# Attention and feed-forward block on one core: units that begin with denominators, and earlier projections for the next batch

## The chip, the cores and the metric

The kernel runs on one core of one Trainium2 chip. The metric is the device time of one execution in microseconds (us), lower is better; before the change the median of three runs is 1805.7 us. The engines are named as the profile names them: PE (TensorE matmuls), PEld (its weight loads), ACT (ScalarE), DVE (VectorE), POOL (GpSimd) and SP (SyncE, which here only issues DMAs).

## What is computed

Eight batches of 1024 tokens with 256 features, 16 heads of 16 features. Cut to what matters, for each batch:

```python
qkv = layernorm(x) @ Wqkv;  q, k, v = split(qkv)           # 16 heads of 16 features
num = exp(rope(q) @ rope(k).T * scale)                      # rotated queries and keys
den = sum(exp(q @ k.T * scale), axis=-1)                    # PLAIN queries and keys, all 1024 columns
attn = where(causal, num / den, 0)
x = x + (attn @ v) @ Wout + bout
x = x + squared_relu(layernorm(x) @ Ws1) @ Ws2 + routed experts(layernorm(x))
```

Numerator and denominator use different scores, so each head needs two score matrices: one from rotated projections (only its causal part) and one from plain ones (all of it). The routed experts get a truncated probability; when the count of tokens with a non-zero one is 0, their loop is skipped.

## The kernel before

**Units and steps.** The work is cut into 32 units: 8 batches (`b`), each with 4 groups of four heads (`g` = 0 to 3, here units one to four of a batch). A unit has 50 steps, written down in `STEPS`. A step is one score tile of 128 x 1024: PE computes it into one of three PSUM tiles (`RING = 3`) and ACT takes its exponential. There are 32 denominator steps, `("den", j, i)` (two matmuls of 512 columns in `scores_step`, the sum along the row by ACT's accumulator), and 18 numerator steps, `("num", c, j)`, in five chunks `c` (four steps each, the last chunk two). PE may compute the tile of step n when ACT has finished that of step n-3 (`exp_done`). Everything is ordered by hand with semaphores; every engine runs its own program in order.

**Side work of PE.** After the score tile of a step PE may do a piece of attention times v (`PV_STEPS`: the step of each of the 12 pieces, function `heads_step`) and one tile of other work (`SIDE`: per unit, step -> kind). The kinds are `v` (value projection), `qk` (projection of the next unit's queries and keys: tiles 0 and 2 are the plain projections of the two halves of the tokens, 1 and 3 the matmul with a swap matrix that the rotation needs), `xt`, `t2` (transposes), `norm`, `acc`, `route`, `ffn`. Tiles in `IN_TWO` take two steps in a row. All side tiles share one PSUM bank, so each waits until DVE has taken the one before (`taken`).

**How queries and keys reach PE.** DVE and POOL split each projected tile into three bf16 parts (`qk_tile` on DVE, `low_part` on POOL, which stands `LOW_LAG = 3` steps behind in POOL's program and sets `low_ready`). SP sends the parts to a scratch tensor in HBM (`send_parts`, `qk_parts<-parts`) and from there fills a stack of 96 rows in SBUF (`fill_stacks`, 12 DMAs for the plain kind and 12 for the rotated kind, `stack<-qk_parts`). There are two stacks by parity of the unit. One semaphore for each parity, `stacked`, counts all 24 fills, and PE waits for all of them ahead of the first step of a unit.

**Order in a unit before.** Four numerators (chunk 0), 7 denominators, chunk 1, 7 denominators, chunk 2, 6, chunk 3, 6, chunk 4, 6 denominators. The next unit's projections run as side work of the present unit; in unit four of a batch they are those of the next batch.

**Outputs.** `send_out(b, g)` waits for `out_ready` and sends two blocks of `x_mid`. Before, the first of a batch stood in SP's program between the two halves of `send_parts`, the second behind its fills, the other two at the end of the batch.

Of the kernel before, what the change touches and what calls it, by code (L numbers as in the profile page):

```python
# [25 lines left out]
HG = 4  # L26
# [10 lines left out]
RING = 3  # L37
Q_TERMS = (0, 0, 0, 1, 1, 2)
K_TERMS = (0, 1, 2, 0, 1, 0)
FILLS = 2 * 2 * TERMS  # L40

# [16 lines left out]

def unit_steps():
    steps, dens = [], [("den", j, i) for j in range(HG) for i in range(NB)]
    for c, count in zip(range(5), (7, 7, 6, 6, 6)):
        steps += [("num", c, j) for j in (range(HG) if c < 4 else range(0, HG, 2))]
        steps += [dens.pop(0) for _ in range(count)]
    return steps

# [2 lines left out]
NSTEP = len(STEPS)  # L70
LAST_STEP = {c: max(s for s, x in enumerate(STEPS) if x[:2] == ("num", c)) for c in range(5)}
FIRST_DEN = next(s for s, x in enumerate(STEPS) if x[0] == "den")

PIECES = [(0, 0), (0, 1), (1, 0), (1, 1), (2, 0), (2, 1), (2, 2), (3, 1), (3, 0), (3, 2), (4, 0), (4, 1)]
PV_STEPS = [
# [4 lines left out]
]  # L82
PV_AT = [dict(zip(steps, PIECES)) for steps in PV_STEPS]
CHUNK_END = [(0, 1), (1, 1), (2, 2), (3, 2), (4, 1)]
# [10 lines left out]


SIDE = [
    {0: ("v", 0), 4: ("v", 1), 9: ("qk", 0), 13: ("v", 2), 16: ("qk", 1), 19: ("qk", 2), 26: ("qk", 3),
     28: ("v", 3)},
    {0: ("qk", 0), 7: ("qk", 1), 11: ("qk", 2), 18: ("qk", 3), 24: ("norm", 0), 26: ("norm", 1),  # L100
     28: ("acc", 0), 29: ("acc", 1), 35: ("acc", 2), 38: ("acc", 3)},
    {0: ("qk", 0), 5: ("t2", 0), 7: ("qk", 1), 8: ("t2", 1), 11: ("qk", 2), 15: ("t2", 2), 17: ("qk", 3),
     19: ("t2", 3), 24: ("route", 0), 25: ("route", 1), 28: ("norm", 0), 31: ("norm", 1), 35: ("acc", 0),
     37: ("acc", 1), 39: ("route", 2), 41: ("acc", 2), 44: ("acc", 3)},
    {0: ("xt", 0), 3: ("xt", 1), 5: ("xt", 2), 8: ("xt", 3), 11: ("qk", 0), 16: ("ffn", 0), 18: ("qk", 1),
     21: ("ffn", 1), 23: ("qk", 2), 28: ("ffn", 2), 31: ("qk", 3), 34: ("ffn", 3), 36: ("ffn", 4),
     38: ("ffn", 5), 41: ("ffn", 6), 45: ("ffn", 7)},
]
IN_TWO = {("v", 0), ("v", 1), ("v", 2), ("v", 3), ("qk", 0), ("qk", 2)}
FFN = [("up", 0), ("up", 1), ("down", 0), ("up", 2), ("down", 1), ("up", 3), ("down", 2), ("down", 3)]  # L110
# [19 lines left out]
def block(nc, x, w_qkv, w_out, b_out, ws1, ws2, w1, w2, wr, cos_in, sin_in, out):  # L130
# [5 lines left out]
    with ExitStack() as ctx:  # L136
# [6 lines left out]
        def sem(name):  # L143
            return ctx.enter_context(nc.semaphore(name))
# [117 lines left out]
        @program.sync  # L262
        def _(sp):
            w_qkv_v = w_qkv.rearrange("(k p) n -> p k n", p=P)
            sp.dma_start(x_in[:, :, :], x_v[0]).then_inc(x_loaded, 16)
            sp.dma_start(stage, w_qkv_v[:, :, 0:2 * D]).then_inc(loaded, 16)
            sp.dma_start(cos_sb[:, :], cos_in).then_inc(tables_loaded, 16)
            sp.dma_start(sin_sb[:, :], sin_in).then_inc(tables_loaded, 16)
            sp.dma_start(w_v[:, :, :], w_qkv_v[:, :, 2 * D:3 * D]).then_inc(more_loaded, 16)
            wo_v = w_out.rearrange("(p a j d) n -> a j d p n", p=2, a=2, j=HG)  # L270
            for a in range(2):
                for j in range(HG):
                    sp.dma_start(w_o[32 * j + DH * a:32 * j + DH * (a + 1), :, :], wo_v[a, j]).then_inc(more_loaded, 16)
# [5 lines left out]
            def send_parts(b, g, outs=None):  # L279

                parity = g % 2

                if not (isinstance(b, int) and b == 0 and g == 0):
                    sp.wait_ge(stacked[1 - parity], at(b, 2 * FILLS * 16, (g + parity) // 2 * FILLS * 16))
                    sp.sem_inc(held["sp"], 1)
                for half in range(2):
                    for kind, sent in ((0, plain_sent), (1, rot_sent)):
                        sp.wait_ge(low_ready, at(b, 16, 4 * g + 2 * half + kind + 1))
                        sp.sem_inc(held["sp"], 1)
                        sp.dma_start(scratch[kind, :, :, :, half * HALF:(half + 1) * HALF].rearrange("c s r t -> (s r) c t"),  # L290
                                     parts[:, kind, :, :]).then_inc(sent, 16)
                        if half == 1:
                            if kind == 0 and not (isinstance(b, int) and b == 0 and g < 2):

                                sp.wait_ge(scores_ready, at(b, G * NSTEP, (g - 1) * NSTEP))
                                sp.sem_inc(held["sp"], 1)
                            fill_stacks(b, g, kind, sent)
                    if outs is not None:
                        send_out(outs, half)

            def fill_stacks(b, g, kind, sent):

                parity = g % 2
                sp.wait_ge(sent, at(b, 8 * 16, 2 * 16 * (g + 1)))
                sp.sem_inc(held["sp"], 1)
                src = scratch[kind].rearrange("c s (d h) t -> c s d (h t)", h=HG)
                for a, terms in enumerate((Q_TERMS, K_TERMS)):
                    for term, part in enumerate(terms):
                        sp.dma_start(stack[term:ROWS:TERMS, parity, kind, a, :], src[part, a]).then_inc(stacked[parity], 16)  # L309

            def batch(b, first, last):
                for g in range(G):
                    if g < G - 1:
                        send_parts(b, g + 1)
                    elif not last:
                        send_parts(b + 1, 0, None if first else b - 1)
# [166 lines left out]
        def _(pe):  # L483
# [139 lines left out]
            def experts(b):  # L623
# [4 lines left out]
                with pe.If(count > 0):  # L628
                    with pe.Fori(0, E) as e:
                        base = at1(b, TILES["gen"], 0) + e * 12  # L630

# [62 lines left out]
            def batch(b, first, last):  # L694

                before = [("qk", b, 3)] + ([] if first else [("ffn", b - 2, TILES["ffn"] - 1)])
                for g in range(G):
                    parity = g % 2
                    pe.wait_ge(stacked[parity], at(b, 2 * FILLS * 16, (g // 2 + 1) * FILLS * 16))
                    for s, step in enumerate(STEPS):  # L700
                        scores_step(b, first, g, s, step)
                        if s in PV_AT[g]:
                            heads_step(b, first, g, s)
                        before = side_step(b, first, last, g, s, before)
                        if (g, s) == BRANCH and not first:

                            for k0, b0, n0 in before:
                                pe.wait_ge(taken[k0], at(b0, TILES[k0], n0 + 1))
                            experts(b - 1)
                            before = before + [("gen", b - 1, TILES["gen"] - 1)]  # L710


# [6 lines left out]
            pe.wait_ge(more_loaded, 16 * MORE_LOADS)  # L719
            batch(0, True, False)  # L720
            with pe.Fori(1, B - 1) as b:
                batch(b, False, False)
# [378 lines left out]
```

## Time and profile before

| | |
|---|---|
| Median of 3 runs | 1805.7 us (1805.3 to 1807.01) |
| The profiled execution | 1806.99 us, its span 1805.4 us |
| ACT busy | 1600.0 us, 89% of the span |
| PE busy | 1543.6 us, 85% |
| DVE, POOL busy | 46%, 28% |
| DMA, mean busy share of 16 engines | 30%, 96 GB/s |
| ACT in the chain that ended last | 22%, PE 27%, issue 31% |

Times in the rows are microseconds, unless marked ns. In a timeline a row is a start, a length, the engine, the source line, the instruction, its output and input with their shapes, and a count of instructions that were merged; the square bracket is how long the engine had been idle and what ended the idle time. The length of a merged matmul row contains the end of the last matmul's pipeline, so what a piece of PE work costs is read from start to start. PEclk is the clock granted to TensorE as a share of full speed: 1.00 is 2.4 GHz, 0.50 is 1.2 GHz.

### The profile page before, as it was taken

To read this page: it belongs to the slowest core of one execution; us is meant where nothing else is said; L and a number is where in the kernel's file an instruction comes from. 1 tells how busy PE (TensorE), PEld (TensorE's weight loads), DVE (VectorE), ACT (ScalarE), POOL (GpSimd) and SP (SyncE) were. 2 spreads that over 40 slices of the span, in tenths; PEclk is the share of its full clock that TensorE was granted. 3 is DMA by queue.
4 is the path that set the end of the run, shared out by engine and by line. 5 is a ranking of instruction groups with operands and counts; after the bars stand their busy time and mean duration, and the time that the engine had idled before them with its cause. 6 is when DMAs were issued, how large, how long until landed. Compare 5 with 4: busy or idle time off the path is not lost.

```text
span 1805.4 us, 29587 instructions
## 1 busy us (share of the span) xinstructions
PE 1543.6 (85%) x8416; PEld 612.0 (34%) x8416; DVE 825.3 (46%) x1824; ACT 1600.0 (89%) x2633; POOL 506.5 (28%) x868
## 2 busy tenths in 40 slices
PE   2688889889898898889988988988988889888985
PEld 1222324233433334233432333433443333423333
DVE  5232433464335653365533644347533565336315
ACT  0599998999899998999979998899989999899990
POOL 3133232231233221332322323224123322133210
PEclk8799999999999999999989999999999999999997
DMA  3234232332333313333223323233133331333300
GB/s 114 88 106 125 91 106 73 103 103 71 122 105 106 117 36 115 111 121 100 83 80 100 120 88 120 83 109 110 58 121 105 124 110 42 105 106 97 97 24 24
DMA packets 95023, 172.44 MB, mean 96 GB/s; under 512 B 15488, under 2 KB 82048, under 8 KB 82560
## 3 DMA queue, kind: packets, MB, share of 16 engines
q1 hardware_dynamic: 94848, 170.33, 30.2%
q8 instruction: 82, 1.34, 0.3%
q14 instruction: 93, 0.76, 0.1%
HBM read 111.55 MB, written 58.72 MB: 94 GB/s over the span
## 4 chain that ended last, share of the span: by engine, by line
issue 31%; PE 27%; ACT 22%; POOL 9%; DVE 6%; SPq 2%; DMA 2%; DVEq 0%; ACTq 0%; POOLq 0%
ACT scores L458 14%; PE scores L500 7%; ACT probs L468 7%; PE y_ps L529 5%; PE scores L507 4%; POOL parts L381 4%; PE side L559 3%; POOL rot L379 3%; SPq L309 2%; PE side L566 2%; POOL x_acc L409 1%; PE side L539 1%; ACT probs L470 1%; PE side L580 1%; PE side L614 1%
## 5 line engine op out<-in xcount | busy, mean ns | idle before, releaser
L458 ACT ACTIVATE scores<-scores 128x1024 f32<-128x1024 f32 x1024 | 1046.7, 1028 | 28.6 <-PE scores L500 27.3
L500 PE MATMUL scores<-stack 96*128 96x512 bf16 x2048 | 584.3, 386 | 59.8 <-ACT probs L468 26.3
L468 ACT ACTIVATE probs<-scores 128x1024 f32<-128x1024 f32 x512 | 490.4, 1026 | 119.2 <-PE scores L507 117.2
L507 PE MATMUL scores<-stack 96*128 96x512 bf16 (+3 forms) x1536 | 335.9, 334 | 89.1 <-DMA stack<-qk_parts 68.6
L529 PE MATMUL y_ps<-probs,v_sb 128*32 128x512 f32 (+3 forms) x3072 | 332.6, 505 | 5.9 <-ACT probs L468 4.8
L371 POOL TENSOR_SCALAR_AFFINE_SELECT probs<-probs 128x256 f32<-128x256 f32 (+1 forms) x640 | 224.7, 378 | 372.9 <-ACT probs L468 219.0
L500 PEld LDWEIGHTS scores<-stack 96*128 96x128 bf16 x2048 | 161.2, 98 | 430.5 <-ACT scores L458 202.2
L507 PEld LDWEIGHTS scores<-stack 96*128 96x128 bf16 x1536 | 124.4, 98 | 357.7 <-ACT scores L458 143.8
L381 POOL TENSOR_TENSOR parts<-rest,parts 128x512 bf16<-128x512 f32 x128 | 148.0, 1156 | 344.8 <-DVE parts L813 338.6
L379 POOL TENSOR_TENSOR rot<-raw,cos_sb 128x512 f32<-128x512 f32 x64 | 90.0, 1407 | 515.3 <-DVEq L826 515.3
L458 ACT ACTIVATION_READ_ACCUMULATOR scores<-scores 128x1 f32 x1024 | 206.2, 201 | 0.0
L559 PE MATMUL side<-xnt,w_qk 128*128 128x512 f32 x248 | 126.8, 592 | 0.0
L825 DVE COPY raw<-side 128x512 f32<-128x512 f32 x62 | 42.9, 691 | 159.5 <-PE side L559 148.8
L529 PEld LDWEIGHTS y_ps<-probs,v_sb 128*32 128x32 f32 x3072 | 60.8, 108 | 144.6 <-issue 116.4
L831 DVE TENSOR_TENSOR rest<-side,sin_sb 128x512 f32<-128x512 f32 x62 | 42.7, 690 | 100.8 <-PE side L566 100.8
L793 DVE COPY v_sb<-side 128x128 f32<-128x128 f32 x128 | 28.2, 283 | 124.5 <-PE side L539 123.5
L863 DVE COPY y_sb<-y_ps 128x512 f32<-128x512 f32 x32 | 21.9, 685 | 137.0 <-PE y_ps L529 137.0
L566 PE MATMUL side<-parts,swap 128*128 128x512 bf16 x186 | 52.1, 389 | 33.5 <-POOL parts L381 23.4
L539 PE MATMUL side<-w_v,xnt 128*128 128x256 f32 x256 | 78.1, 434 | 0.0
L809 DVE TENSOR_TENSOR rest<-raw,parts 128x512 f32<-128x512 f32 x64 | 71.9, 1124 | 5.2 <-issue 0.5
L580 PE MATMUL side<-w_o,y_sb 128*128 128x256 f32 x240 | 63.7, 387 | 2.6 <-DVE x_mid L882 2.5
L470 ACT ACTIVATE probs<-scores 128x1024 f32<-128x1024 f32 x64 | 63.0, 1036 | 1.4 <-PE scores L507 1.3
(110 smaller groups left out, 1116.9 us busy)
## 6 DMA issues: line engine op xcount, KB each, us to landing
stack<-qk_parts SPq DMA_DIRECT2D x768, 128.0 KB, 2.6
qk_parts<-parts SPq DMA_DIRECT2D x128, 384.0 KB, 2.6
x_in<-in_L_attn_x SPq DMA_DIRECT2D x8, 1024.0 KB, 5.5
out<-x_mid SPq DMA_DIRECT2D x32, 256.0 KB, 2.8
probs<-in_L_attn_Wqkv SPq DMA_DIRECT2D x1, 512.0 KB, 6.7
cos_sb<-in_cos SPq DMA_DIRECT2D x1, 512.0 KB, 7.4
sin_sb<-in_sin SPq DMA_DIRECT2D x1, 512.0 KB, 8.3
w_v<-in_L_attn_Wqkv SPq DMA_DIRECT2D x1, 256.0 KB, 8.0
```

What stands on the lines that cost most here:

```text
L371: nc.gpsimd.affine_select(out=v, in_=v, compare_op=ALU.is_ge, fill=0.0, base=0, pattern=pattern, channel_multiplier=-1).then_inc(masked, 1)
L379: nc.gpsimd.tensor_tensor(rot[:, :], raw[:, :], cos_sb[:, t // 2 * HALF:(t // 2 + 1) * HALF], ALU.mult)
L381: nc.gpsimd.tensor_tensor(parts[:, t % 2, 2, :], rest[:, :], parts[:, t % 2, 1, :], ALU.subtract).then_inc(low_ready, 1)
L458: nc.scalar.activation(src, src, ACT.Exp, scale=SCALE, accum_out=den[:, g % 2, i, j:j + 1]).then_inc(exp_done, 1)
L468: nc.scalar.activation(probs[:, chunk % 2, j, :], src, ACT.Exp, scale=SCALE).then_inc(exp_done, 1)
L500: mm = nc.tensor.matmul(tile[:, half * HALF:(half + 1) * HALF], q[:, j, i * P:(i + 1) * P], k[:, j, half * HALF:(half + 1) * HALF], start= ...
L507: mm = nc.tensor.matmul(tile[:, col:col + n], k[:, h, i * P:(i + 1) * P], q[:, h, q0:q0 + n], start=True, stop=True)
L529: mm = nc.tensor.matmul(y_ps[32 * j:32 * j + 32, o0:o0 + n], v_sb[:, i, h, :, :], probs[:, (5 * g + c) % 2, j, col:col + n], start=piece i ...
L539: mm = nc.tensor.matmul(side[:, i * D:(i + 1) * D], xnt[:, k, (2 * t + i) * P:(2 * t + i + 1) * P], w_v[:, k, :], start=k == 0, stop=k == ...
L559: mm = nc.tensor.matmul(side, w_qk[:, k, g, :], xnt[:, k, half * HALF:(half + 1) * HALF], start=k == 0, stop=k == KC - 1)
L566: mm = nc.tensor.matmul(side, swap[:, :], parts[:, 0, i, :], start=i == 0, stop=i == PARTS - 1)
L580: mm = nc.tensor.matmul(side[:, i * D:(i + 1) * D], y_sb[:, pair, (2 * t + i) * P:(2 * t + i + 1) * P], w_o[:, pair, :], start=True, stop= ...
```

## The change

`FILLS` counts the fills of one stack (12), and each kind and parity has its own semaphore. PE waits for the plain stack ahead of a unit's first denominator and for the rotated stack ahead of its first numerator. The unit's order becomes 7 denominators, the 8 numerators of chunks 0 and 1, 7 denominators, and from there as before; only steps 0 to 10 differ. The pieces of chunks 0 and 1 in `PV_STEPS` and most of `SIDE` are moved. SP sends all four outputs behind the fills. The waits ahead of the experts' branch stand inside the branch.

```diff
-FILLS = 2 * 2 * TERMS
+FILLS = 2 * TERMS
...
-    for c, count in zip(range(5), (7, 7, 6, 6, 6)):
-        steps += [("num", c, j) for j in (range(HG) if c < 4 else range(0, HG, 2))]
+    for chunks, count in zip(((), (0, 1), (2,), (3,), (4,)), (7, 7, 6, 6, 6)):
+        steps += [("num", c, j) for c in chunks for j in (range(HG) if c < 4 else range(0, HG, 2))]
         steps += [dens.pop(0) for _ in range(count)]
...
 PV_STEPS = [
-    (6, 11, 21, 22, 30, 32, 34, 39, 42, 43, 47, 49),
...
+    (13, 16, 19, 22, 30, 32, 34, 39, 42, 43, 47, 49),
...
 SIDE = [
-    {0: ("v", 0), 4: ("v", 1), 9: ("qk", 0), 13: ("v", 2), 16: ("qk", 1), 19: ("qk", 2), 26: ("qk", 3),
-     28: ("v", 3)},
...
+    {0: ("qk", 0), 3: ("v", 0), 6: ("v", 1), 9: ("qk", 1), 11: ("qk", 2), 14: ("v", 2), 17: ("qk", 3), 20: ("v", 3)},
...
-    {0: ("xt", 0), 3: ("xt", 1), 5: ("xt", 2), 8: ("xt", 3), 11: ("qk", 0), 16: ("ffn", 0), 18: ("qk", 1),
-     21: ("ffn", 1), 23: ("qk", 2), 28: ("ffn", 2), 31: ("qk", 3), 34: ("ffn", 3), 36: ("ffn", 4),
-     38: ("ffn", 5), 41: ("ffn", 6), 45: ("ffn", 7)},
+    {0: ("xt", 0), 2: ("xt", 1), 5: ("xt", 2), 7: ("xt", 3), 9: ("qk", 0), 12: ("ffn", 0), 15: ("qk", 1),
+     17: ("qk", 2), 20: ("ffn", 1), 22: ("ffn", 2), 24: ("qk", 3), 27: ("ffn", 3), 30: ("ffn", 4),
+     33: ("ffn", 5), 36: ("ffn", 6), 39: ("ffn", 7)},
...
-        stacked = [sem("stacked0"), sem("stacked1")]
+        plain_stacked = [sem("plain_stacked0"), sem("plain_stacked1")]
+        rot_stacked = [sem("rot_stacked0"), sem("rot_stacked1")]
...
-                    pe.wait_ge(stacked[parity], at(b, 2 * FILLS * 16, (g // 2 + 1) * FILLS * 16))
                     for s, step in enumerate(STEPS):
+                        if s == FIRST_DEN:
+                            pe.wait_ge(plain_stacked[parity], at(b, 2 * FILLS * 16, (g // 2 + 1) * FILLS * 16))
+                        if s == FIRST_NUM:
+                            pe.wait_ge(rot_stacked[parity], at(b, 2 * FILLS * 16, (g // 2 + 1) * FILLS * 16))
...
-                    for pair in range(0 if last else 2, G):
+                    for pair in range(G):
                         send_out(b - 1, pair)
```

In unit three (not shown) `t2` 2 and 3 move from steps 15 and 19 to 15 and 21 and `qk` 3 from 17 to 19, so the swap no longer stands two steps behind a `t2` tile but four; in unit two `qk` 1 moves from 7 to 8. The first two pieces of attention times v stand at steps 13 and 14 to 16 in every unit, where they stood at 6 to 8 and 10 or 11; those of chunk 1 stand at 17 to 22.

The first place is PE's program at the start of a batch in the loop; L493 and L491 are the wait lines, `stack` the filled stack, `side` the shared bank. Before:

```order
L493 ISA [waits stacked0]
L507 MATMUL scores<-stack 128x512 [waits exp_done]
L507 MATMUL scores<-stack 128x512
L675 ISA
L675 ISA [waits qk_taken]
L539 MATMUL side<-w_v,xnt 128x256 [waits ffn_taken]
```

And now the same place, and behind it the first numerator step of that unit:

```order
L724 ISA
L491 ISA [waits plain_stacked0]
L498 MATMUL scores<-stack 128x512 [waits exp_done]
L498 MATMUL scores<-stack 128x512
L676 ISA
```

```order
L537 MATMUL side<-w_v,xnt 128x256
L488 REGISTER_ALU [waits rot_stacked0]
L505 MATMUL scores<-stack 128x512 [waits exp_done]
L505 MATMUL scores<-stack 128x512
L537 MATMUL side<-w_v,xnt 128x256 x2
```

The first step is a denominator (L498) behind 12 fills; the numerator (L505) and the other 12 fills stand at step 7.

The second place is SP's program in unit four of the loop, from the first send of parts to the fills. Before:

```order
L290 DMA qk_parts<-parts 128x3x512 [waits low_ready]
L326 ISA
L328 ISA [waits out_ready]
L328 DMA out<-x_mid 128x2x256
L288 REGISTER_ALU
L290 DMA qk_parts<-parts 128x3x512 [waits low_ready]
L295 ISA
L304 ISA [waits scores_ready]
L309 DMA stack<-qk_parts 16x4096 [waits plain_sent]
L309 DMA stack<-qk_parts 16x4096 x11
```

Now:

```order
L290 DMA qk_parts<-parts 128x3x512 [waits low_ready]
L288 REGISTER_ALU
L290 DMA qk_parts<-parts 128x3x512 [waits low_ready]
L295 ISA
L302 ISA [waits scores_ready]
L307 DMA stack<-qk_parts 16x4096 [waits plain_sent]
L307 DMA stack<-qk_parts 16x4096 x11
```

The output, and its wait for `out_ready`, no longer stand between the halves; the four outputs follow the rotated fills.

The third place is PE's program in unit one, steps 11 to 16 (shown from the first batch, where no register instructions stand between). Before:

```order
L507 MATMUL scores<-stack 128x512 x2
L529 MATMUL y_ps<-probs,v_sb 32x512 x4
L507 MATMUL scores<-stack 128x512 x4
L539 MATMUL side<-w_v,xnt 128x256 x2
L507 MATMUL scores<-stack 128x512 x2
L539 MATMUL side<-w_v,xnt 128x256 x2
L500 MATMUL scores<-stack 128x512 x4
L566 MATMUL side<-parts,swap 128x512 x3
```

Now:

```order
L557 MATMUL side<-xnt,w_qk 128x512
L505 MATMUL scores<-stack 128x512 x2
L557 MATMUL side<-xnt,w_qk 128x512
L505 MATMUL scores<-stack 128x512 x2
L527 MATMUL y_ps<-probs,v_sb 32x512 x4
L505 MATMUL scores<-stack 128x512 x2
L537 MATMUL side<-w_v,xnt 128x256 x2
L498 MATMUL scores<-stack 128x512 x2
L537 MATMUL side<-w_v,xnt 128x256 x2
L498 MATMUL scores<-stack 128x512 x2
L527 MATMUL y_ps<-probs,v_sb 32x512 x4
```

Before, a step without side work stood between most pieces; now every step from 11 to 17 carries one.

## Rows read from the trace of the kernel before

**Rows 1.** Waits of ACT over the whole span, the largest two before the tail
```profile
ACT probs L468 <- PE scores L507: 117.2, 72, 50.2
...
ACT scores L458 <- PE scores L500: 27.3, 51, 2.4
```

**Rows 2.** Windows of 14 us at the seven batch boundaries, ACT, their sum
```profile
sum 98.00, ACT 45.45; mean ACT 6.49
```

**Rows 3.** Timeline of ACT around the boundary of the fourth and fifth batch
```profile
888.97 3.74 ACT L468 ACTIVATE probs<-scores 128x1024 f32<-128x1024 f32 x4
892.58 1.04 ACT L458 ACTIVATE scores<-scores 128x1024 f32<-128x1024 f32 x1
...
893.61 1.03 ACT L458 ACTIVATE scores<-scores 128x1024 f32<-128x1024 f32 x1
...
906.30 1.00 ACT L458 ACTIVATE scores<-scores 128x1024 f32<-128x1024 f32 x1
...
914.14 1.02 ACT L468 ACTIVATE probs<-scores 128x1024 f32<-128x1024 f32 x1 [6.72 <-PE scores L507]
```

**Rows 4.** Timeline of SP (DMA issues) at the same boundary
```profile
889.44 7.85 SPq L309 DMA_DIRECT2D stack<-qk_parts  x12
897.49 0.43 SPq L290 DMA_DIRECT2D qk_parts<-parts  x1
900.35 7.97 SPq L309 DMA_DIRECT2D stack<-qk_parts  x12
```

**Rows 5.** Timeline of POOL, the last low part ahead of that boundary
```profile
891.15 1.16 POOL L381 TENSOR_TENSOR parts<-rest,parts 128x512 bf16<-128x512 f32 x1 [4.45 <-DVE parts L813]
```

**Rows 6.** Timeline of PE, end of unit four and first tile of the next batch
```profile
893.74 0.60 PE L500 MATMUL scores<-stack 96*128 96x512 bf16 x2
894.18 1.03 PE L614 MATMUL side<-xn2t,ws_sb 128*128 128x256 f32 x4
895.05 0.60 PE L500 MATMUL scores<-stack 96*128 96x512 bf16 x2
...
897.88 0.60 PE L507 MATMUL scores<-stack 96*128 96x384 bf16 x4
898.41 1.06 PE L529 MATMUL y_ps<-probs,v_sb 128*32 128x512 f32 x8
899.41 0.61 PE L507 MATMUL scores<-stack 96*128 96x384 bf16 x4
...
912.99 1.03 PE L507 MATMUL scores<-stack 96*128 96x512 bf16 x2 [7.59 <-DMA stack<-qk_parts]
```

**Rows 7.** Timeline of SP at the start of the program, the plain fills
```profile
42.23 7.53 SPq L309 DMA_DIRECT2D stack<-qk_parts  x12
```

**Rows 8.** Timeline of PE at the start, its first score tile
```profile
62.45 1.01 PE L507 MATMUL scores<-stack 96*128 96x512 bf16 x2 [21.42 <-DMA stack<-qk_parts]
```

**Rows 9.** Timeline of ACT at the start, its first exponentials
```profile
63.50 1.02 ACT L468 ACTIVATE probs<-scores 128x1024 f32<-128x1024 f32 x1 [50.16 <-PE scores L507]
65.81 1.02 ACT L468 ACTIVATE probs<-scores 128x1024 f32<-128x1024 f32 x1 [1.28 <-PE scores L507]
```

**Rows 10.** Timeline of ACT, unit one of the fourth batch, step 23
```profile
726.40 2.85 ACT L468 ACTIVATE probs<-scores 128x1024 f32<-128x1024 f32 x3 [0.30 <-PE scores L507]
```

**Rows 11.** Timeline of PE, unit three of the fourth batch, step 17
```profile
823.71 0.81 PE L566 MATMUL side<-parts,swap 128*128 128x512 bf16 x3 [1.52 <-DVE xn2t L892]
824.35 1.03 PE L500 MATMUL scores<-stack 96*128 96x512 bf16 x4
```

**Rows 12.** Timeline of ACT, the step behind it
```profile
824.99 1.01 ACT L458 ACTIVATE scores<-scores 128x1024 f32<-128x1024 f32 x1 [1.37 <-PE scores L500]
```

**Rows 13.** Windows of PE in unit two of the fifth batch: busy, PEclk, DMA share, GB/s
```profile
974.00:976.00 2.00, 2.00 (x5) 0.50 0.59 197
```

**Rows 14.** Timeline of PE just ahead of that window
```profile
972.69 0.60 PE L500 MATMUL scores<-stack 96*128 96x512 bf16 x2 [0.42 <-ACT scores L458]
```

**Rows 15.** Timeline of ACT behind it
```profile
979.05 1.01 ACT L458 ACTIVATE scores<-scores 128x1024 f32<-128x1024 f32 x1 [1.72 <-PE scores L500]
```

More of the change, by code:

```diff
@@ L72 @@
 FIRST_DEN = next(s for s, x in enumerate(STEPS) if x[0] == "den")
+FIRST_NUM = next(s for s, x in enumerate(STEPS) if x[0] == "num")
 PIECES = [(0, 0), (0, 1), (1, 0), (1, 1), (2, 0), (2, 1), (2, 2), (3, 1), (3, 0), (3, 2), (4, 0), (4, 1)]
 PV_STEPS = [
[4 rows of a table removed]
[4 rows of a table added]
 ]
@@ L97 @@
 SIDE = [
-    {0: ("v", 0), 4: ("v", 1), 9: ("qk", 0), 13: ("v", 2), 16: ("qk", 1), 19: ("qk", 2), 26: ("qk", 3),
-     28: ("v", 3)},
-    {0: ("qk", 0), 7: ("qk", 1), 11: ("qk", 2), 18: ("qk", 3), 24: ("norm", 0), 26: ("norm", 1),
+    {0: ("qk", 0), 3: ("v", 0), 6: ("v", 1), 9: ("qk", 1), 11: ("qk", 2), 14: ("v", 2), 17: ("qk", 3), 20: ("v", 3)},
+    {0: ("qk", 0), 8: ("qk", 1), 11: ("qk", 2), 18: ("qk", 3), 24: ("norm", 0), 26: ("norm", 1),
      28: ("acc", 0), 29: ("acc", 1), 35: ("acc", 2), 38: ("acc", 3)},
-    {0: ("qk", 0), 5: ("t2", 0), 7: ("qk", 1), 8: ("t2", 1), 11: ("qk", 2), 15: ("t2", 2), 17: ("qk", 3),
-     19: ("t2", 3), 24: ("route", 0), 25: ("route", 1), 28: ("norm", 0), 31: ("norm", 1), 35: ("acc", 0),
+    {0: ("qk", 0), 4: ("t2", 0), 7: ("qk", 1), 9: ("t2", 1), 11: ("qk", 2), 15: ("t2", 2), 19: ("qk", 3),
+     21: ("t2", 3), 25: ("route", 0), 26: ("route", 1), 29: ("norm", 0), 31: ("norm", 1), 35: ("acc", 0),
      37: ("acc", 1), 39: ("route", 2), 41: ("acc", 2), 44: ("acc", 3)},
-    {0: ("xt", 0), 3: ("xt", 1), 5: ("xt", 2), 8: ("xt", 3), 11: ("qk", 0), 16: ("ffn", 0), 18: ("qk", 1),
-     21: ("ffn", 1), 23: ("qk", 2), 28: ("ffn", 2), 31: ("qk", 3), 34: ("ffn", 3), 36: ("ffn", 4),
-     38: ("ffn", 5), 41: ("ffn", 6), 45: ("ffn", 7)},
+    {0: ("xt", 0), 2: ("xt", 1), 5: ("xt", 2), 7: ("xt", 3), 9: ("qk", 0), 12: ("ffn", 0), 15: ("qk", 1),
+     17: ("qk", 2), 20: ("ffn", 1), 22: ("ffn", 2), 24: ("qk", 3), 27: ("ffn", 3), 30: ("ffn", 4),
+     33: ("ffn", 5), 36: ("ffn", 6), 39: ("ffn", 7)},
 ]
@@ L277, in _, with send_parts @@
             sp.dma_start(wr_sb[:, :, 0:E], wr.rearrange("(k p) e -> p k e", p=P)).then_inc(more_loaded, 16)
-            def send_parts(b, g, outs=None):
+            def send_parts(b, g):
                 parity = g % 2
-                if not (isinstance(b, int) and b == 0 and g == 0):
-                    sp.wait_ge(stacked[1 - parity], at(b, 2 * FILLS * 16, (g + parity) // 2 * FILLS * 16))
-                    sp.sem_inc(held["sp"], 1)
                 for half in range(2):
-                    for kind, sent in ((0, plain_sent), (1, rot_sent)):
+                    for kind, sent, stacked in ((0, plain_sent, plain_stacked), (1, rot_sent, rot_stacked)):
+                        if half == 0 and not (isinstance(b, int) and b == 0 and g == 0):
+                            sp.wait_ge(stacked[1 - parity], at(b, 2 * FILLS * 16, (g + parity) // 2 * FILLS * 16))
+                            sp.sem_inc(held["sp"], 1)
                         sp.wait_ge(low_ready, at(b, 16, 4 * g + 2 * half + kind + 1))
@@ L296, in send_parts, with fill_stacks @@
                                 sp.sem_inc(held["sp"], 1)
[L297 to L301, printed above, removed]
+                            fill_stacks(b, g, kind, sent, stacked)
+            def fill_stacks(b, g, kind, sent, stacked):
                 parity = g % 2
@@ L315, in batch @@
                     elif not last:
-                        send_parts(b + 1, 0, None if first else b - 1)
+                        send_parts(b + 1, 0)
                     if g == 1 and not last:
@@ L621, in ffn_tile, with experts @@
                 mm.then_inc(full["ffn"], 1)
-            def experts(b):
+            def experts(b, before=()):
                 pe.wait_ge(routed_ready, at(b, 1, 1))
@@ L628, in experts @@
                 with pe.If(count > 0):
+                    for k0, b0, n0 in before:
+                        pe.wait_ge(taken[k0], at(b0, TILES[k0], n0 + 1))
+                        pe.sem_inc(held["pe"], 1)
                     with pe.Fori(0, E) as e:
@@ L705, in batch @@
                         if (g, s) == BRANCH and not first:
-                            for k0, b0, n0 in before:
-                                pe.wait_ge(taken[k0], at(b0, TILES[k0], n0 + 1))
-                            experts(b - 1)
+                            experts(b - 1, before)
                             before = before + [("gen", b - 1, TILES["gen"] - 1)]
@@ L719, in _ @@
             pe.wait_ge(more_loaded, 16 * MORE_LOADS)
+            pe.wait_ge(taken["qk"], 4)
             batch(0, True, False)
```

6 rows, old and new, of the table PV_STEPS are left out of this document.

## The prediction

> **What bounds the kernel now.** On the page ACT is busy for 89% of the span and PE for 85%, so ACT's exponentials set the pace and PE has little to spare. The first view to read is the waits of ACT: numerators waited 117.2 us and denominators 27.3 us for PE's score tiles [rows 1]. Of the 117.2 us, 50.2 us are the start of the program. The rest has to be placed, and the windows of ACT at the seven batch boundaries do that: 98.00 us of windows hold 45.45 us of work, so 52.5 us are idle there [rows 2]. What is left, 144.5 - 50.2 - 52.5 = 42 us, is spread over the 32 units, about 1.3 us each.
>
> The timeline shows why a boundary costs so much. ACT finishes its last denominator at 907.3 us and gets its first numerator at 914.14, 6.72 us later [rows 3]; PE had stood 7.59 us for the stack [rows 6], so it had been ready at 905.4. Back from there: POOL had the last rotated part ready at 892.31 [rows 5], but SP, in order, was still issuing the 12 plain fills (7.85 us) and sent that part at 897.49; its fills ran from 900.35 to 908.32 [rows 4], and PE began 4.7 us after the last of them was issued. The plain fills ended at 897.3: with the same 4.7 us they had landed by 902.0, before PE was ready.
>
> **The change, part by part.**
>
> *Boundaries.* With denominators first, PE needs the plain stack at 905.4 and the rotated one seven steps later, at 905.4 + 7 x 1.03 = 912.6 (a denominator takes 893.61 - 892.58 = 1.03 us of ACT, a numerator (892.58 - 888.97)/4 = 0.90 us [rows 3]). Even with nothing else moved, 912.99 would leave a wait of 0.4 us. The last plain projection also moves from steps 23 and 24 to 17 and 18, the last swap from 31 to 24. So the plain fills end some 6 us earlier, at 891.3; the last rotated part, ready at 885, is sent then; 2.9 us later the fills begin, take 8 us, end near 902.1 and have landed by 906.8, almost 6 us ahead of need. The output wait that stood between the halves is gone from SP's path; outputs are now behind the fills, where only the next batch's first parts follow, some five steps later, and DVE's wait for the outputs stands in unit two, step 28; were that cover gone, their issue (about 0.4 us each) would be the price. All seven waits go, with the slow first steps behind them: **-52.5 us**.
>
> *Start.* The plain fills are issued by 49.8 us [rows 7]. From the end of the rotated fills (60.3) PE needed 2.2 us to begin at 62.45 [rows 8]; so it now begins at about 52, and seven denominators (7.2 us of ACT), even stretched by matmuls at half clock, are done at about 63. The rotated stack is there at 62.4, as before, and the first numerator falls at 63.5 as before [rows 9]. Gained are the 7.2 us of denominators and most of the 1.28 us and smaller waits that followed the first tile: **-8 us**.
>
> *Nothing gained at other unit starts.* There the stacks are in time today; a second semaphore wait on PE costs no time that a row shows. The number of exponentials, matmuls and DMAs is unchanged. The waits moved into the experts' branch are not met when the count is 0, and the next side tile has them anyway: 0.
>
> *Denser side work.* This is the price. Costs from start to start [rows 6]: a pair of score matmuls 0.44 us, an fp32 side tile or half 0.87, a pair ahead of a piece of attention times v 0.53, that piece 1.00; a swap 0.64 [rows 11]. PE can be a limited time ahead. I calibrate how far at one spot: in unit one, steps 19 to 22 (two projection halves, two pieces) ask 4 x 0.43 + 2 x 0.87 + 2 x 1.08 = 5.6 us of PE while ACT needs 3 x 1.03 + 0.90 = 4.0, and ACT waits 0.30 us at step 23 [rows 10]; the lead is 1.6 - 0.3 = 1.3 us.
>  - Unit one, steps 11 to 22, now holds six fp32 halves, a swap and four pieces: 12 x 0.43 + 6 x 0.87 + 0.65 + 4 x 1.08 = 15.3 us against ACT's 5 x 0.90 + 7 x 1.03 = 11.7. Less the lead, 2.3 us of waiting, where this unit waits 0.9 us today (0.30 and two like it): +1.4 us, eight times, **+11 us**.
>  - Unit four, steps 9 to 22, now holds four projection halves, three `ffn` tiles, a swap and four pieces: 14 x 0.43 + 7 x 0.87 + 0.65 + 4 x 1.08 = 17.1 against 7 x 0.90 + 7 x 1.03 = 13.5; 2.3 us of waiting against 0.2 today. In the six batches that have both kinds: **+12 us**.
>  - Unit three: the swap waited 1.52 us for the `t2` tile that DVE had not yet taken, and ACT waited 1.37 us behind it [rows 11, 12]. With four steps between them instead of two that is gone, in seven batches -9.6 us; two pieces behind the projection at steps 11 to 14 give back about 0.3 us each: **-7.5 us**.
>  - Unit two: side work moves by a step, a piece from 8 to 13; **0**, between -1 and +3 us in all.
>
> *The clock.* In unit two of the fifth batch the granted clock fell to 0.50 of full speed, the lower level [rows 13], behind a stretch of score pairs alone whose gaps were 0.42 us [rows 14]; ACT then waited up to 1.72 us in one piece [rows 15], 2.7 us in all with its neighbours. Such a stretch now comes in unit one, steps 23 to 29 (no side work), and at the start of units two to four of sparse batches. The boundaries, where the clock fell every time, no longer do that, which is in the 52.5. I take two more such spells than today: **+5 us**.
> The Trainium skill (TensorE: Matmul & The Clock Gate, "Why this matters for your kernels") puts throttling down to idle gaps between bursts of matmuls. By it the change could only raise the clock, since it removes the long gaps, and this term would be 0 and the forecast 5 us lower. These rows show a fall without such a gap, so I keep the term.
>
> **Sum.** 1805.4 - 52.5 - 8 + 11 + 12 - 7.5 + 5 = 1765.4 us of span. The median of the runs stands 0.3 us above that span (1805.7), though the profiled run's own time was 1806.99. Forecast: **1766 us**.
>
> **Bounds.** Boundaries: -45 (a wait of 1 us stays at each) to -53. Start: -5 to -9. The dense stretches: from 0 net (PE's lead larger than at my one spot, interlocks gone) to +35 (each adds a wait for DVE or POOL of up to 0.8 us, since the swap now stands nearer behind its projection). Clock: -2 to +20.
>
> **Rivals.**
>  1. *The dense stretches cost next to nothing.* PE's lead may be larger in a row of denominators, whose tiles are all written ahead. Then the terms +11, +12 and half the clock's fall away: about 1741 to 1750 us. Against it: the calibration is a measured wait, and demand above pace for twelve steps must show. Chance 0.19.
>  2. *The clock falls in unit one of each batch and again at a second sparse stretch.* Two spells of 2.7 us in each of eight batches, 43 us, less some 13 for today's: +30 instead of my +5, 1791 us. For it: rows 13 to 15. Against: pieces at half clock delay only where they stand close together, and steps 30 to 34 hold three. Chance 0.13.
>  3. *Slower than before.* If the clock fell at each unit's start, where now up to 13 denominators follow one another, and hit the dense steps 11 to 22 at half clock, a spell costs not 2.7 but the whole lead and more. The net gain of 40 us is used up from 15 spells of 2.7 us on; with 32, one in each unit, 1766 + 86 - 5 = 1847. Against it: the boundary units of today run five bare steps in a row as well, and the fall of rows 13 is the exception there. Chance 0.02.
>  4. *The change does not do what it says:* the rotated stack is late at step 7 by as much as today. It would need SP or POOL to be 13 us later than worked out; then the 52.5 us are missing from the sum, 1818 us, or with half of them 1792. Chance 0.03.
>
> The forecast has 0.63; its own range is 1754 to 1780. The range for 8 in 10 takes in rival 1's upper part and some of rival 2: 1746 to 1784. A measurement of this kernel tells about 0.2% (3.6 us) from no change; faster by more 0.95, within it 0.01, slower 0.04 (rival 3 and two thirds of 4).
>
> **What the profile after would show.** No wait of PE for `stack` at the boundaries, ACT's first exponential near 53 us and its first numerator near 63.5, the wait of 1.37 us in unit three gone; instead more ACT waits of 0.2 to 0.6 us around steps 13 to 22 in units one and four, some 4.5 us a batch. In the windows of PE, 0.50 in places behind bare score pairs. The prediction is wrong if those dense steps run without waits (then it is too high), if a wait on `stack` shows at step 7, or if the clock falls in most units.

## The result and the profile after

The changed kernel takes 1852.6 us (median of four runs, 1850.67 to 1854.44) against 1806.4 us before: a ratio of 1.026, 95% interval 1.024 to 1.028. It is 46 us slower, where 40 us faster had been forecast.

First the page of the changed kernel: the span, the engines and the groups of ACT and of the first matmul, in the page's own columns.

```profile
span 1850.6 us, 29626 instructions
...
PE 1604.7 (87%) x8416; PEld 612.8 (33%) x8416; DVE 824.5 (45%) x1824; ACT 1608.2 (87%) x2633; POOL 507.7 (27%) x868
...
L456 ACT ACTIVATE scores<-scores 128x1024 f32<-128x1024 f32 x1024 | 1042.1, 1021 | 111.6 <-PE scores L498 109.7
...
L466 ACT ACTIVATE probs<-scores 128x1024 f32<-128x1024 f32 x512 | 490.4, 1025 | 85.1 <-PE scores L505 84.5
```

ACT's work is nearly the same (1608 us of busy time against 1600, in the same 2633 instructions), so almost all of the 45 us by which the span grew are waits. The numerators wait less than in [rows 1] (84.5 against 117.2 us, and none of it is the start any more), the denominators four times as much (109.7 against 27.3 us, of which 50.6 are now the start).

To see where, I took from ACT's timeline every interval between two denominators and subtracted what the pace of [rows 3] gives for it (1.03 us for the denominator, 0.905 for each numerator in between). What is left is the excess: all waits, also those too short for a bracket. Numerators that stand ahead of a denominator are counted with it. Mean per batch, batches two to seven, in us:

```
                                      before   after
unit one, without its first two steps   1.6      6.1
unit two                                2.5      1.9
unit three                              3.0      2.6
unit four, steps 0 to 14                0.3      7.4
unit four, steps 15 to 48               0.9      3.2
boundary (last step and first two)      8.1      3.6
sum                                    16.4     24.8
```

Eight more each batch, some 50 us in six batches, against about 10 us gained at the start. Three places carry it.

**Unit four, step 12.** The timeline of the changed kernel in the fifth batch, PE, then DVE, then ACT:

```profile
1101.22 1.03 PE L505 MATMUL scores<-stack 96*128 96x512 bf16 x4
1105.92 2.07 PE L612 MATMUL side<-xn2t,ws_sb 128*128 128x256 f32 x4 [3.68 <-DVEq L977]
1107.79 1.06 PE L505 MATMUL scores<-stack 96*128 96x512 bf16 x2
1108.78 1.94 PE L527 MATMUL y_ps<-probs,v_sb 128*32 128x512 f32 x8
```

```profile
1101.58 0.69 DVE L828 COPY raw<-side 128x512 f32<-128x512 f32 x1 [3.24 <-PE side L557]
1102.41 0.43 DVE L810 CAST parts<-raw 128x512 bf16<-128x512 f32 x1
1102.91 1.59 DVE L812 TENSOR_TENSOR rest<-raw,parts 128x512 f32<-128x512 f32 x1
1104.58 0.43 DVE L816 CAST parts<-rest 128x512 bf16<-128x512 f32 x1
```

```profile
1108.89 1.02 ACT L466 ACTIVATE probs<-scores 128x1024 f32<-128x1024 f32 x1 [4.87 <-PE scores L505]
1111.72 1.02 ACT L466 ACTIVATE probs<-scores 128x1024 f32<-128x1024 f32 x1 [1.81 <-PE scores L505]
```

The `ffn` tile of step 12 stood 3.68 us. Its releaser, `DVEq L977`, is no computation: it is DVE's queue raising `taken["gen"]` in the empty side of the experts' branch, which stands behind step 10 (`BRANCH = (3, 10)`). Before, DVE had only the short copy of `xt` tile 3 ahead of that branch, and the chain of `qk` tile 0 began behind it, as its timeline in the same unit of the kernel before shows:

```profile
1080.84 0.69 DVE L800 COPY xnt<-side 128x512 f32<-128x512 f32 x1 [2.72 <-PE side L548]
1085.99 0.69 DVE L825 COPY raw<-side 128x512 f32<-128x512 f32 x1 [4.45 <-PE side L559]
```

Now `qk` tile 0 stands ahead of the branch (step 9), and DVE works through its whole chain, 1101.58 to 1105.0, before it gets there. The waits of PE in the changed kernel (total, count, largest) hold this one six times:

```profile
PE side L612 <- DVEq L977: 22.4, 6, 4.0
```

PE's clock was at its lower level (1.2 GHz) after the pause, as the next window shows, and two more waits of ACT follow. (Columns: stretch, its length, PE busy, count, PEclk, DMA share, GB/s.)

```profile
1106.00:1108.00 2.00, 2.00 (x5) 0.50 0.41 135
```

**The boundary.** PE and SP of the changed kernel between the fifth and sixth batch:

```profile
1149.03 0.42 PE L527 MATMUL y_ps<-probs,v_sb 128*32 128x128 f32 x8
1152.81 0.93 PE L498 MATMUL scores<-stack 96*128 96x512 bf16 x2 [3.36 <-issue]
1153.53 1.92 PE L557 MATMUL side<-xnt,w_qk 128*128 128x512 f32 x2
```

```profile
1139.67 5.65 SPq L307 DMA_DIRECT2D stack<-qk_parts  x9
1145.68 2.50 SPq L326 DMA_DIRECT2D out<-x_mid  x4
```

The wait for the stack of [rows 6] is gone: the last rotated fill was issued by 1145.3 (the row takes in the last nine of twelve), as the prediction had it, and PE did not wait for `stack` again after the start. Yet PE stood 3.36 us, and the releaser is "issue", nothing that the profile shows. At the five boundaries inside the loop it stood 2.8 to 3.4 us (3.21, 2.88, 2.82, 3.36 and 2.94); two of the five are put down to "issue", the other three to ACT's tile, which had come before. What lies there is the jump back of PE's loop over batches (its back edge). Between the first and the second batch, where PE runs into the loop from code written out, it waits only for ACT, 1.1 us, so that some 2 us of each longer pause are the jump's:

```profile
265.39 0.60 PE L498 MATMUL scores<-stack 96*128 96x512 bf16 x2 [1.09 <-ACT scores L456]
```

**Unit one.** It has no single long wait, but many of 0.2 to 0.7 us at steps 13 to 23, in every batch, and one at step 31, where the kernel before waited too (0.42 us).

### The profile page after: what moved, and what is told of

Read it like the earlier page. It is cut to its first block, busy times and chain, and to the rows that moved or that the text cites. A ratio compares the mean times of both kernels' runs of the same rounds, so it can differ in the third digit from the quotient of the medians.

```text
span 1850.6 us, 29626 instructions
## 1 busy us (share of the span) xinstructions
PE 1604.7 (87%) x8416; PEld 612.8 (33%) x8416; DVE 824.5 (45%) x1824; ACT 1608.2 (87%) x2633; POOL 507.7 (27%) x868
## 4 chain that ended last, share of the span: by engine, by line
issue 34%; PE 26%; ACT 23%; DVE 8%; POOL 7%; DVEq 1%; DMA 1%; POOLq 0%; SPq 0%; ACTq 0%
ACT scores L456 17%; PE scores L498 6%; PE y_ps L527 6%; ACT probs L466 5%; PE scores L505 5%; POOL parts L379 4%; POOL rot L377 2%; PE side L557 2%; PE side L537 2%; DVE rest L812 2%; PE side L578 1%; DVE parts L810 1%; ACT probs L468 1%; DVE raw L828 1%; POOL probs L369 1%
## 5 line engine op out<-in xcount | busy, mean ns | idle before, releaser
L456 ACT ACTIVATE scores<-scores 128x1024 f32<-128x1024 f32 x1024 | 1042.1, 1021 | 111.6 <-PE scores L498 109.7
L498 PE MATMUL scores<-stack 96*128 96x512 bf16 x2048 | 596.7, 391 | 102.1 <-ACT scores L456 61.8
L466 ACT ACTIVATE probs<-scores 128x1024 f32<-128x1024 f32 x512 | 490.4, 1025 | 85.1 <-PE scores L505 84.5
L505 PE MATMUL scores<-stack 96*128 96x512 bf16 (+3 forms) x1536 | 354.3, 346 | 32.1 <-ACT scores L456 25.7
L527 PE MATMUL y_ps<-probs,v_sb 128*32 128x512 f32 (+3 forms) x3072 | 342.8, 519 | 0.0
L498 PEld LDWEIGHTS scores<-stack 96*128 96x128 bf16 x2048 | 159.7, 99 | 500.5 <-ACT scores L456 260.2
L505 PEld LDWEIGHTS scores<-stack 96*128 96x128 bf16 x1536 | 125.7, 100 | 322.5 <-ACT scores L456 118.2
L456 ACT ACTIVATION_READ_ACCUMULATOR scores<-scores 128x1 f32 x1024 | 201.1, 196 | 0.0
L557 PE MATMUL side<-xnt,w_qk 128*128 128x512 f32 x248 | 137.9, 639 | 6.0 <-DVE xn2t L895 6.0
L537 PE MATMUL side<-w_v,xnt 128*128 128x256 f32 x256 | 68.1, 388 | 4.3 <-DVE v_sb L796 2.1
L810 DVE CAST parts<-raw 128x512 bf16<-128x512 f32 x64 | 64.1, 1002 | 8.7
L868 DVE TENSOR_TENSOR y_sb<-y_ps,y_sb 128x512 f32<-128x512 f32 x32 | 21.9, 684 | 95.9 <-PE y_ps L527 95.9
```

Source lines behind the costliest of these rows:

```text
L456: nc.scalar.activation(src, src, ACT.Exp, scale=SCALE, accum_out=den[:, g % 2, i, j:j + 1]).then_inc(exp_done, 1)
L466: nc.scalar.activation(probs[:, chunk % 2, j, :], src, ACT.Exp, scale=SCALE).then_inc(exp_done, 1)
L498: mm = nc.tensor.matmul(tile[:, half * HALF:(half + 1) * HALF], q[:, j, i * P:(i + 1) * P], k[:, j, half * HALF:(half + 1) * HALF], start= ...
L505: mm = nc.tensor.matmul(tile[:, col:col + n], k[:, h, i * P:(i + 1) * P], q[:, h, q0:q0 + n], start=True, stop=True)
L527: mm = nc.tensor.matmul(y_ps[32 * j:32 * j + 32, o0:o0 + n], v_sb[:, i, h, :, :], probs[:, (5 * g + c) % 2, j, col:col + n], start=piece i ...
L537: mm = nc.tensor.matmul(side[:, i * D:(i + 1) * D], xnt[:, k, (2 * t + i) * P:(2 * t + i + 1) * P], w_v[:, k, :], start=k == 0, stop=k == ...
```

## The experiments

Ratios are to the kernel before, with their 95% intervals; since the chips differ a little (beside the three groups of experiments the kernel before took 1805.5, 1811.1 and 1812.4 us), experiments of different groups are compared by ratio. The first group is `e1` to `e4`, the second `e5` to `e8`, the third `e9` to `e11`.

**The branch, the loop, and both.** In the changed kernel:

```diff
-BRANCH = (3, 10)
+BRANCH = (3, 8)
```

and, by itself and together with it, in the program of PE alone:

```diff
-            with pe.Fori(1, B - 1) as b:
+            for b in range(1, B - 1):
                 batch(b, False, False)
```

> The changed kernel with one constant moved: the experts' branch stands behind step 8 of unit four, ahead of the first projection (step 9), instead of behind step 10. Theory A (a wait behind DVE): in unit four PE stands 3.7 us ahead of the ffn tile of step 12, because that tile waits for the semaphore that DVE raises only in its branch, and DVE has its whole 3.4 us projection chain of step 9 ahead of the branch. ACT loses some 7.2 us between steps 7 and 14 there in six batches. With the branch ahead of the projection that goes: about 6 us a batch, 36 to 40 us in all, 1812 to 1816 us. Rival B (too dense side work alone, as my prediction had it): the stall is there because PE cannot keep up; moving the branch changes nothing, 1848 to 1853 us. Rival C (the branch itself costs PE and DVE their time wherever it stands): the stall moves to step 8 or 9, 1840 to 1850 us.

Measured: 1818.2 us, ratio 1.006 (1.004 to 1.009), from 1.026: 34 us less, and 2 us over the expected range. The excess in unit four, steps 0 to 14, fell from 7.4 to 1.6 us. PE at the same `ffn` tile of the fifth batch, without a wait:

```profile
1084.26 1.03 PE L505 MATMUL scores<-stack 96*128 96x512 bf16 x4
1085.37 1.13 PE L612 MATMUL side<-xn2t,ws_sb 128*128 128x256 f32 x4
```

Theory A holds, and rivals B and C do not: one constant, the place of a branch that does nothing in this run, was worth 34 us.

> The changed kernel with PE's loop over batches written out, all else alike. Theory D (the loop's back edge): at five of the seven boundaries, those that jump back in the loop, PE stands 3.4 us at 'issue' ahead of its first tile, and ACT loses 3 to 5 us with the cold clock behind it; the boundaries into and out of the loop have next to nothing. Before the change that time lay under the wait for the stack. Written out, five times 3.5 to 4.5 us go: 17 to 22 us, 1829 to 1835 us. Rival (the time is that of fetching new instructions, loop or not, or of a wait not shown): it stays, 1848 to 1853 us.

Measured: 1830.5 us, ratio 1.015 (1.011 to 1.019), 20 us less by the ratios (22 by the medians). The same boundary, PE:

```profile
1135.60 0.43 PE L527 MATMUL y_ps<-probs,v_sb 128*32 128x128 f32 x8
1137.21 0.59 PE L498 MATMUL scores<-stack 96*128 96x512 bf16 x2 [1.19 <-ACT scores L456]
```

PE now waits for ACT, as it should, and its clock is up (0.59 for two matmuls that took 0.93). Theory D holds for the changed kernel.

> The kernel before with PE's loop over batches written out, the control for the run above. Theory D with its cover: at each boundary PE waits for the stack until later than the back edge takes, so nothing is gained: within 3 us of before, 1803 to 1808 us. Rival (the back edge is paid in full there too): five times 3.4 us less, 1787 to 1791 us.

Measured: 1803.0 us, ratio 0.999 (0.997 to 1.001). The same edit that gives 20 us in the changed kernel gives nothing measurable in the one before; its PE waits for the stack almost as long as it did (68.6 us before):

```profile
PE scores L507 <- DMA stack<-qk_parts: 67.0, 15, 21.3
```

The back edge was there before and lay under that wait.

> The changed kernel with both edits, branch behind step 8 and PE's loop written out. If theories A and D are both right and independent, the savings add: 1852 less 38 less 20, 1792 to 1798 us, which would be just faster than before. What then remains over my forecast of 1766 us is the denser side work, some 28 us. Rival: the two stalls hide each other or share the cold clock, and the sum is under 45 us saved, over 1805 us.

Measured: 1795.0 us, ratio 0.993 (0.991 to 0.996). 57.6 us less than the changed kernel, about the sum of the two (34 and 22): two independent stalls. It is the first version faster than before.

**Denominators first, with the old side work.** `STEPS`, the semaphores and the outputs as changed, `SIDE` as before, the pieces of chunks 0 and 1 at 13 or later:

```diff
 PV_STEPS = [
+    (15, 17, 21, 22, 30, 32, 34, 39, 42, 43, 47, 49),
     (13, 15, 17, 22, 32, 33, 36, 39, 42, 43, 47, 49),
+    (13, 14, 16, 20, 30, 32, 34, 39, 42, 43, 47, 49),
+    (13, 14, 17, 20, 30, 32, 37, 39, 42, 43, 47, 49),
 ]
 SIDE = [            # as in the kernel before
```

> One part of the change alone: denominators first, a semaphore for each stack and the outputs behind the fills, but the side work (SIDE) of the kernel before, with the branch behind step 10; the pieces of attention times v must stay at 13 or later, since chunk 0 is done only then (units one, three and four at 15, 17, 21, 22; 13, 14, 16, 20; 13, 14, 17, 20). Theories A and D: at the boundaries only PE's back edge is left (5 times some 4 us), the branch stands right behind a short DVE copy as before, so no stall at step 12, and the projections need not be early, since the rotated stack is wanted only at step 7. Start gains 8 us. 1805 less 52 less 8, plus 20 for the edge, plus up to 20 for pieces crowded into steps 13 to 22: 1775 to 1795 us. Rival (the late projections keep the stack late at step 7, as the move was meant to prevent): 1800 us and over, with PE waits for the stack of several us at step 7 of each batch.

Measured: 1771.0 us, ratio 0.977 (0.975 to 0.979), 4 us under the expected range. PE's waits between 100 and 1790 us hold none for the stack, at step 0 or 7; of its boundaries only the loop's edge shows, here under "issue" at three of the five (the other two pauses, 2.7 and 3.0 us, are put down to ACT):

```profile
PE scores L499 <- issue: 10.3, 3, 3.6
```

So the order of the unit and the second semaphore were right, and the projections need not have been moved at all. The whole loss sits in the moved side work and its pieces.

> The run above with PE's loop over batches written out. Theory D: 17 to 22 us less than it, 1757 to 1775 us. Rival (the stack at step 7 is late anyway and covers the edge): within 5 us of it.

Measured: 1750.5 us, ratio 0.967 (0.965 to 0.968): 20 us less again, the difference expected; the time lies under the range given, as that of its base did.

**Density.** On the base of 1795 us. Unit one alone:

```diff
-    {0: ("qk", 0), 3: ("v", 0), 6: ("v", 1), 9: ("qk", 1), 11: ("qk", 2), 14: ("v", 2), 17: ("qk", 3), 20: ("v", 3)},
+    {0: ("qk", 0), 3: ("v", 0), 6: ("v", 1), 10: ("qk", 1), 17: ("qk", 2), 24: ("qk", 3), 26: ("v", 2), 28: ("v", 3)},
...
-    (13, 16, 19, 22, 30, 32, 34, 39, 42, 43, 47, 49),
+    (13, 15, 20, 22, 31, 32, 35, 39, 42, 43, 47, 49),
```

> The same base of 1795 us, but only unit one spread: its projections at steps 0, 10, 17 and 24, its last two value tiles at 26 and 28, pieces at 13, 15, 20, 22, 31, 32, 35. Tells what unit one alone costs by density: its excess over the pace of ACT alone is 5.8 us a batch, of which some 2.5 should remain; 8 times 3.3, 22 to 28 us less, 1767 to 1773 us. Rival as above: under 8 us less.

Measured: 1769.2 us, ratio 0.977 (0.976 to 0.979): 26 us less (29 by the ratios), and unit one's excess from 5.8 to 2.4 us. For unit one the sum of demand against pace is a good guide.

Then unit four too (`qk` at 9, 14, 17, 24, `ffn` at 26, 28, 30, 33, 35, 37, 40, 45, pieces at 13, 16, 20, 22, 31, 32, 36):

> The changed kernel with the branch behind step 8 and PE's loop written out (1795 us), and the side work of units one and four spread so that PE's demand, added up from the rows, exceeds ACT's pace by less than PE's lead of 1.3 us at every place. My arithmetic of density: unit one loses some 3.5 us less, unit four 3 us less, together 40 to 50 us over eight batches: 1747 to 1760 us. Rival (what is left over my forecast is not density but clock and interlocks): under 15 us less, over 1780 us.

Measured: 1782.9 us, ratio 0.984 (0.982 to 0.986), 14 us slower than with unit one alone, where 1747 to 1760 us had been expected; the rival's 1780 and over is what came. The waits of PE for its swap tiles show most of the reason, in this run and then in the one with only unit one spread:

```profile
PE side L564 <- POOL parts L379: 20.4, 22, 2.2
```

```profile
PE side L564 <- POOL parts L379: 4.9, 10, 1.7
```

I had put the swap at step 14, four steps behind the projection halves of 9 and 10. DVE's and POOL's chain from the end of the projection to the low part takes 5.0 us (in the changed kernel above, PE ends at 1101.22, and the low part at 1106.2), and those four steps are numerators of 0.9 us. PE stood 1.8 to 2.2 us for the swap in seven units of this run. Unit four's excess there (steps 7 to 21) is some 1.6 us a batch above the other run's; another 1 us comes later, at steps 29 to 44, where the `ffn` tiles and the pieces now stand together. My arithmetic adds up PE's demand and knows no such distance; it was wrong where a distance, not the load, decides.

Last, on the 1750 us version, value tile 2 of unit one from 13 to 23 and its pieces at 13, 15, 18, 22, 31:

> The 1750 us version with one tile and five pieces of unit one moved: value tile 2 from steps 13, 14 to 23, 24, pieces at 13, 15, 18, 22 instead of 15, 17, 21, 22, one from 30 to 31. By demand against pace the waits in steps 15 to 22 (1.9 us a batch) go and 0.6 us come at 23, 24: 8 to 11 us less, 1740 to 1743 us. Rival (the tiles' own waits for DVE and POOL, which the sum of demand leaves out, decide): within 4 us, or slower.

Measured: 1746.8 us, ratio 0.964 (0.962 to 0.966) against 0.967 (0.965 to 0.968): the intervals overlap, and the medians are 3.7 us apart. The excess of unit one fell from 2.0 to 1.3 us a batch, not to 0.8. That is half the expectation, and within the 4 us of its rival; the run does not decide between them. By its median it is the fastest version, 3.6% faster than before. What is left of ACT's waits there, with 50.2 of the first row being the start:

```profile
ACT scores L457 <- PE scores L499: 71.1, 46, 50.2
...
ACT probs L467 <- PE scores L506: 22.8, 66, 0.9
```

**The other loops, and the outputs.**

> The 1750 us version (denominators first, side work of before, PE's loop written out) with the loops of ACT, DVE, POOL and SP written out too. Theory D for the other engines: ACT loses another 0.7 us at each boundary, the other engines' back edges are covered; 3 to 6 us less, 1744 to 1748 us. Rival (PE's was the only one exposed): within 3 us. Rival (fetching the longer program costs): slower by over 3 us.

Measured: 1754.0 us, ratio 0.968 (0.967 to 0.970) against 0.967 (0.965 to 0.968): no gain that can be measured, against 3 to 6 us expected. One thing did change in the profiled runs. In the 1750 us version ACT stands at five of the boundaries inside its loop for nothing that the profile shows, and this line of its waits is gone when the loops are written out:

```profile
ACT scores L457 <- issue: 2.5, 5, 0.7
```

So ACT's edge was exposed as well, by some 2 us in all, too little to show in the median. PE's is the only one whose price can be measured.

> The kernel before with one part of the change alone: all four outputs of a batch behind the fills. The output wait that stood ahead of the last plain part ended at about the moment that part was ready, so nothing is late by it: within 4 us of before. Rival (the wait delays the plain fills, and through SP's order the rotated ones): up to 1 us at each of seven boundaries earlier, 1798 to 1802 us against 1805. Against both: outputs closer to the next batch could slow the last fills' landing, up to 7 us more.

Measured: 1812.9 us, ratio 1.0005 (0.998 to 1.003): no effect, as expected. This was tried in the kernel before only.

## Why the prediction was wrong, step by step

The measured sizes below are the excesses of the two profiled runs, summed over all eight batches and not only over the six of the table.

- *Start: -8.* Right, slightly small. The first exponential is at 52.82 us and the first numerator at 62.96; some 10 us gained. From ACT's timeline of the changed kernel, the first row:

```profile
52.82 1.01 ACT L456 ACTIVATE scores<-scores 128x1024 f32<-128x1024 f32 x1 [50.60 <-PE scores L498]
```

- *Boundaries: "all seven waits go", -52.5.* The mechanism was right: the rotated fills were issued by 1145.3, and no wait for the stack came back. The size was not: the seven boundaries together went from 55 to 21 us of excess, -34 us, since at the five boundaries inside the loop PE's back edge, a pause of 2.8 to 3.4 us and a slow clock behind it, had lain under the wait for the stack. The step that failed is taking ACT's whole idle time there as the stack's doing; I had asked what hides an added cost, not what the removed wait had been hiding. The Trainium skill has a rule for such a jump (Runtime: NRT & Kernel Launch, "Instruction fetch mechanics"): a taken branch whose target is outside the engine's current pages forces a fetch of the target before it can go on. The runs agree by effect, 20 us for five jumps, and show nothing of the mechanism itself.
- *"The waits moved into the experts' branch are not met ... and the next side tile has them anyway: 0."* This is the step that failed worst. The next side tile has them, and that was the trouble: the tile of step 12 waits for DVE's branch, and the move had put a DVE chain of 3.4 us ahead of it. Measured +34 us. I had asked what the removed waits were worth, and not what stands ahead of the instruction that releases the next one. The order of DVE's program was there to read.
- *Denser side work, unit one: +11.* Right in mechanism and place, a third of the true size: 6.1 us a batch against 1.6, +33 us in all with the clock's share; spreading it gave 26 back. Two errors: I let the stretch begin with the full lead of 1.3 us at step 11, while steps 6 to 10 had used some of it (the numerators of 7 to 14 alone lose 2.5 us), and I counted today's waits by their brackets (0.9) where the excess is 1.6 and of the new ones only what exceeded the lead. These two are read off the traces and were not tested one by one.
- *Unit four: +12.* Too small by half: steps 15 to 48 rose by 2.3 us a batch and the numerators of 7 to 14, without the branch, by 1.3, +26 us in all (unit four rose by 60 us, of which the branch is 34).
- *Unit three: -7.5.* The wait behind the `t2` tile did go, but the numerators of steps 7 to 14 lose 2.2 us now, so 1.5 us were gained. The term also took back 0.3 us a batch where its own text has 0.3 us for each of two pieces, which would have made it -5.4. *Unit two: 0.* It gained some 3 us.
- *The clock: +5.* It fell more often than the term allows. Between 63 and 1750 us of the profiled runs it stood at 0.50 in 31 stretches, 150 us in all, against 15 and 96 us before. In unit one of the first seven batches it fell at step 27 or 28, in the stretch of score pairs alone where the prediction had placed it; it fell as well at step 4 or 5 of unit two in the same seven batches (before, in two of them), and behind each pause at step 12 of unit four and at the loop's edge. The windows of PE at the first two places in the sixth batch, and the piece that was hit in unit one:

```profile
1188.00:1190.00 2.00, 2.00 (x10) 0.50 0.66 234
1216.00:1218.00 2.00, 2.00 (x6) 0.50 0.58 194
```

```profile
1188.93 1.82 PE L527 MATMUL y_ps<-probs,v_sb 128*32 128x512 f32 x8
```

  At steps 31 to 35 ACT waited 0.3 to 0.6 us in four of the six batches and 2.4 and 2.6 us in two, where it had waited 0.42 us before. What the clock cost is inside the excess of units one and two and was not tested by itself, so the size of this term stays open. Of the Trainium skill's rule on the clock gate (TensorE: Matmul & The Clock Gate, "Why this matters for your kernels"), idle gaps between bursts, this trace bears out one half: the clock fell behind all eleven pauses of 2.8 to 4.0 us at those two places. It does not cover the other falls: the gaps ahead of the one in unit one were 0.25 to 0.41 us.

Rival 3 named the right side, by a mechanism that was not the cause: the clock fell in three units of four, but with the falls in units one and two still there `e4` is 57.6 us faster. Its 1847 us are near the measured time by accident. The sum by the measured terms is 1805.4 - 10 - 34 + 34 (the branch) + 33 + 26 - 2 - 3 + 1 (the end of the program) = 1850, against a span of 1850.6.

Two parts of the change were good (the order of the unit with its second semaphore: 2.3% or some 40 us faster by themselves, 3.3% or 60 us with the loop written out), one was neutral (outputs), and the moved side work cost some 80 to 90 us: 1852.6 against 1771.0 us, ratio 1.026 against 0.977.

What stays open: how much of the excess of units one and two the clock alone makes, and what PE's time at the back edge consists of.

## What to carry to other kernels

When a wait is to be removed, ask what else it covers: look at the same place where that cost would be absent (here the boundary into the loop against those inside it), and try the edit that would remove the hidden cost on the kernel before, where it must give nothing. When work is moved on one engine, read the order of every engine that shares a semaphore with it: an instruction that only raises a semaphore, in a branch that does nothing, is as late as the longest work moved ahead of it. Adding up an engine's demand against the pace finds crowded stretches, but the distance between producer and consumer through the other engines (5 us here) is a second condition, and work should not be moved earlier than it is needed.

## What the runs showed of the hardware

- At PE's jump back over a body of 1052 matmuls it stood still for 2.8 to 3.4 us, where it stands 1.1 to 1.2 us for ACT without the jump. The profile names no releaser ("issue") or puts the pause down to ACT. Five of them with the clock behind them cost some 20 us. The jumps of the other four engines cost nothing that the median shows; ACT's shows in the trace with 2.5 us in five.
- Each of the eleven pauses of 2.8 to 4.0 us on PE at step 12 of unit four and at the loop's edge was followed by the lower clock (0.50), and so were the seven of 1.8 to 2.2 us in `e7_spread`. The pause of 3.7 us cost ACT some 5.8 us, 4.87 us at once and the rest behind it.
- Writing out PE's loop six times over had no price that shows: the first exponential came at 52.83 us against 52.82, and the ratio was 0.999 where it could gain nothing.
